# The last level of a block solve: GpSimd adds the unit matrix instead of 16 identity products on TensorE

## The chip, the cores and the metric

The kernel runs on one core of a Trainium2 chip. The metric is the device time of one launch in microseconds (us), lower is better. One core has TensorE (PE, with its weight loads shown as PEld), VectorE (DVE), ScalarE (ACT), GpSimd (POOL) and SyncE (SP), each with its own in-order queue of instructions, and they synchronise by semaphores.

## The reference

A two-layer decoder over 32 items (batch entries) of 128 tokens by 128 channels. Only one part touches the change: the second layer's linear attention with 16 heads of 64 channels. In it the recurrence over the 64 tokens of a chunk,

```
S = S * a_t[:, :, None]
kTS = einsum('bd,bde->be', k_t, S)
S = S + (b_t * k_t)[:, :, None] * (v_t - kTS)[:, None, :]
```

is not run token by token. The kernel solves the unit lower triangular system (I - N) W = V per head, with N strictly lower triangular of size 64, as a product of factors: W = (I + N^32) (I + N^16) ... (I + N) V. That is six levels, k = 0 to 5. Level k needs N^(2^k); step X{k} makes the next power by squaring and step W{k} multiplies W by (I + N^(2^k)).

## The kernel before, in words

The kernel has three blocks one after the other (first layer, a quantised feed-forward part that finds its scales, second layer). The third block, from about 1170 us to the end, holds the change. Two items are in flight, called lane 0 and lane 1, half a round apart; 16 rounds serve 32 items. Each lane has its own buffers, 4 PSUM banks and semaphores. Every engine's queue is written out in full by a fixed list of 0s and 1s (`CSLOTS`) that says which lane gives its next stage; no scheduler decides anything at run time. So an engine that waits in one lane's stage also holds up the other lane's stages behind it.

The 16 heads are handled as 8 pairs, and `tiles()` gives 16 products of 64x64 per step. An f32 product is two matrix instructions in the profile, each with its own weight load, so 16 products are rows with x32.

Where the change sits, in the order of TensorE's queue in lane 0: X4 (line 1203, last squaring), then for lane 1 the norm's product (L1010), W4 and KmT (L1217, L1221), for lane 1 one filler product (L353, `keep_warm`, products with no use that keep TensorE busy) and "conv" (L1109), then A (L1238), W5 (L1227 and L1229), then lane 1's "alpha" (L1115, L1117), which waits for DVE's L1512 ("c4m"). In lane 1 the order is X4, W4, KmT, lane 0's "fc" (L1306), A, lane 0's "pj" (L1312), W5, lane 0's "y" (L1100), fillers, and lane 0's last norm (L1007), which waits for DVE's L1600.

At levels 0 to 4 GpSimd forms I + N^(2^k) in SBUF (`with_identity`, L995, buffer `TI`) and TensorE multiplies once. At level 5 TensorE multiplies twice into one PSUM sum: N^32 times W (L1227) and the identity times W (L1229).

DVE's work in lane 1 that belongs to "conv" and "inner" is a convolution with 4 taps over three buffers: L1481 (`tensor_scalar`, SBUF to SBUF, two per-partition scalars, x3), L1507 ("zm", reads PSUM), L1483 (`scalar_tensor_tensor`, two SBUF tensors in, x6), then L1512. GpSimd's other instruction in this block is L458 ("Kbd", once per item).

Of the kernel before, what the change touches and what calls it, by code (L numbers as in the profile page):

```python
# [32 lines left out]
DK = 64  # L33
# [117 lines left out]
def decoder(nc, a):  # L151
    with ExitStack() as ctx:
# [12 lines left out]
        ident = sb("ident", [P, P])  # L165
# [70 lines left out]
        for s in range(LANES):  # L236
            n = Lane()
# [108 lines left out]
        mm = nc.tensor.matmul  # L346
# [122 lines left out]
        def sigmoid(act, ph, it, s, name, cols):  # L469
# [17 lines left out]
        LEVELS = 6  # L487
        y_pe, y_act, y_dve, y_pool = attention_steps("y")
# [12 lines left out]
             "Qd0", "Qd1", "Km0", "Kp0", "Km1", "Kp1", "t2", "cc", "dd", "Mm", "P0", "cV0", "cV1", *[f"X{k}" for k in range(LEVELS - 1)],  # L501
             "AT0", "AT1", "S", "ve", "f", "ON0", "ON1", "xs", "lng", "qmask", "yq", *y_dve, "ys", "lny", "fr2",
             *[f"ls{i}" for i in range(1, 6)], "lx", "lnf"],
            [*[f"TI{k}" for k in range(LEVELS - 1)], *y_pool])


        w_raw = lane[0].Kbd[:, 0:2 * FT, :]
# [87 lines left out]
        pe_did, act_did, dve_did, pool_did, loaded, stored = ph.pe, ph.act, ph.dve, ph.pool, ph.loaded, ph.stored  # L595
# [383 lines left out]
        def tiles():  # L979

            for j in range(NP // 2):
                for p in (j, j + NP // 2):
                    for lo, hi in halves:
                        other = (DK - lo, P + DK - hi) if p >= NP // 2 else (lo, hi)
                        yield p, slice(lo, hi), slice(*other)

        def groups():

            order = list(tiles())
            return [order[k:k + 4] for k in range(0, len(order), 4)]  # L990
# [30 lines left out]
        with nc.Block() as block:  # L1021
# [27 lines left out]
            @block.gpsimd  # L1049
            def _(pool):  # L1050
                def advance(s, it, stage):
                    n = lane[s]
                    if stage == "T0":
                        pool.wait_ge(pc.act[s], pc.AC.upto(it, "T0"))
                        with_identity(pool, it, s, 0)
                    for k in range(LEVELS - 2):
                        if stage == f"X{k}":
                            pool.wait_ge(pc.act[s], pc.AC.upto(it, f"X{k}"))
                            pool.wait_ge(pc.dve[s], pc.DV.upto(it, f"X{k}"))
                            if k > 0:  # L1060
                                pool.wait_ge(pc.pe[s], pc.PE.upto(it, f"W{k - 1}"))
                            with_identity(pool, it, s, k + 1)
                    if stage == "yKbd":
                        pool_attention(pool, pc, it, s, "y", pc.PE.upto(it, "O1"))
                in_rounds(pool, advance, CSLOTS["pool"])

            @block.tensor
            def _(pe):
                def advance(s, it, stage):
                    n, b = lane[s], lane[s].bank  # L1070
# [4 lines left out]
                    def dve_did(name):  # L1075
                        pe.wait_ge(pc.dve[s], pc.DV.upto(it, name))
# [14 lines left out]
                    if stage == "h":  # L1091
                        keep_warm(b[3], CWARM["h"])
                        pe.wait_ge(pc.loaded[s], 16 * C_LOADS * (it + 1))
                        for j in range(FT):
                            last = mm(b[3][:, j * P:(j + 1) * P], w1_q[:, j, :], n.xq[:, 0, :], start=True, stop=True)
                        last.then_inc(pf.pe[s], pf.PE.step(s, "h"))
                    if stage == "y":
                        pe.wait_ge(pf.dve[s], pf.DV.upto(it, "hq2"))
                        for j in range(FT):
                            last = mm(b[3][:, 0:P], w2_q[:, j, :], n.hq[:, j * P:(j + 1) * P], start=(j == 0), stop=(j == FT - 1))  # L1100
# [20 lines left out]
                    if stage == "F":  # L1121
                        keep_warm(b[0], CWARM["F"])
                        act_did("aE1")
                        for i in range(2):
                            act_did(f"aL{i}")
                            for p in range(4 * i, 4 * i + 4):
                                last = mm(pair_out(p, 2), n.B[:, p, :], since[:, :], start=True, stop=True)  # L1127
# [7 lines left out]
                    def held():  # L1135
                        pe.sem_inc(pe_passed, 1)

                    def solve_out(p, at, bank, col=0, width=DK):
                        first = (p % 4) * width + col
                        return n.psum[at, bank + p // 4, first:first + DK]  # L1140

                    if stage == "ssq":
# [3 lines left out]
                        for odd in range(2):  # L1146
                            for j in range(4):
                                p = 2 * j + odd
                                last = mm(b[0][QR * j:QR * (j + 1), 0:2 * P], hsel[:, p, :], squares[:, p, :, :], start=(odd == 0), stop=(odd == 1))
# [38 lines left out]
                    for k in range(LEVELS):  # L1188

                        PT, W = (n.PT0, n.PT1)[k % 2], n.W if k > 0 else n.cV[:, 0, :, :]  # L1190
                        if stage == f"X{k}":
                            if k == 0:
                                act_did("T0")
                            else:
                                act_did(f"X{k - 1}")
                                dve_did(f"X{k - 1}")
                            held()
                            for group in groups():
                                if k < LEVELS - 2:
                                    for p, src, dst in group:  # L1200
                                        mm(solve_out(p, dst, 2, 0, P), PT[src, p, 1, :], PT[src, p, 0, :], start=True, stop=True)  # L1201
                                for p, src, dst in group:
                                    last = mm(solve_out(p, dst, 2, DK, P), PT[src, p, 0, :], PT[src, p, 1, :], start=True, stop=True)  # L1203
                            last.then_inc(pc.pe[s], pc.PE.step(s, f"X{k}"))
                        if stage == f"W{k}":
                            if k == 0:
                                dve_did("cV1")
                            elif k < LEVELS - 1:
                                act_did(f"W{k - 1}")
                            else:  # L1210
                                act_did("KmT")
                                dve_did(f"X{k - 1}")
                            if k < LEVELS - 1:
                                pe.wait_ge(pc.pool[s], pc.PO.upto(it, f"TI{k}"))
                                held()
                                for p, src, dst in tiles():
                                    last = mm(solve_out(p, dst, 0), n.TI[src, k % 2, p, :], W[src, p, :], start=True, stop=True)  # L1217
                                last.then_inc(pc.pe[s], pc.PE.step(s, f"W{k}"))
                                if k == LEVELS - 2:
                                    for p, src, dst in tiles():  # L1220
                                        last = mm(solve_out(p, dst, 0, 4 * DK), n.Km[src, p, 0:DK], ident[src, src], start=True, stop=True)  # L1221
                                    last.then_inc(pc.pe[s], pc.PE.step(s, "KmT"))
                                continue
                            held()
                            for group in groups():
                                for p, src, dst in group:
                                    mm(solve_out(p, dst, 0), PT[src, p, 1, :], W[src, p, :], start=True, stop=False)  # L1227
                                for p, src, dst in group:
                                    last = mm(solve_out(p, dst, 0), ident[src, src], W[src, p, :], start=False, stop=True)  # L1229
                            last.then_inc(pc.pe[s], pc.PE.step(s, f"W{k}"))  # L1230
                    if stage == "A":
                        act_did(f"X{LEVELS - 2}")
                        dve_did(f"X{LEVELS - 2}")
# [481 lines left out]
```

## Time and profile before

| what | value |
|---|---|
| time of 3 runs | 2942.89 us median (2939.81 to 2944.56) |
| the profiled execution, its own time | 2953.11 us |
| its span in the trace | 2951.3 us |
| PE busy | 2614.6 us, 89% of the span (104.6 of 110.0 us from 2184 to 2294, a round of the third block) |
| DVE, ACT busy | 1669.5 us (57%), 1640.9 us (56%) |
| POOL busy | 305.0 us (10%), of it L995 202.7 us in 160 instructions |
| granted TensorE clock, mean | 0.98 |

Shares of busy time are means over stages; what ends a wait at one place is read from the rows. In such rows "idle before <- who" is the time the engine did nothing before the instruction and what released it; "issue" means that nothing in the profile held it, as when its next instructions had not arrived.

### The profile page before, as it was taken

How to read it: one execution, taken by the hardware profiler on the slowest of the kernel's cores; microseconds unless marked ns; L12 is line 12 of the kernel's file. 1: busy time of each engine (PE TensorE's matmuls, PEld its weight loads, DVE VectorE, ACT ScalarE, POOL GpSimd, SP SyncE). 2: the span in 40 equal slices, each digit the busy share in tenths (PEclk: the TensorE clock that was granted, in tenths of full speed). 3: DMA queues.
4: the chain of work that ended last, by engine and by line, in shares of the span. 5: the costliest groups of instructions: out<-in, count | busy, mean ns of one | idle time of the engine just before them, and what ended most of it. 6: DMA issues, size and time to landing. Idle time of an engine off the chain costs nothing.

```text
span 2951.3 us, 94478 instructions
## 1 busy us (share of the span) xinstructions
PE 2614.6 (89%) x41924; PEld 1885.5 (64%) x41928; DVE 1669.5 (57%) x3917; ACT 1640.9 (56%) x3841; POOL 305.0 (10%) x270
## 2 busy tenths in 40 slices
PE   3888888888888865999999999999999999998997
PEld 1665655566565543777776766777777777766775
DVE  3556656655665655456555465555556556555563
ACT  2655655655565532565565555555565565565563
POOL 0000000000000000111111111111111111111111
PEclk9999999999999986999999999999999999999999
DMA  3000000000000001000000000000000000000000
GB/s 98 6 8 6 6 9 7 6 6 8 6 6 9 6 22 29 6 6 8 7 6 8 7 6 8 7 6 8 7 5 8 7 6 8 7 5 8 7 6 4
DMA packets 50654, 29.21 MB, mean 10 GB/s; under 512 B 19792, under 2 KB 48528, under 8 KB 50256
## 3 DMA queue, kind: packets, MB, share of 16 engines
q1 hardware_dynamic: 50256, 23.25, 2.8%
q8 instruction: 330, 5.41, 0.8%
q14 instruction: 68, 0.56, 0.1%
HBM read 17.98 MB, written 5.24 MB: 8 GB/s over the span
## 4 chain that ended last, share of the span: by engine, by line
PE 47%; ACT 6%; DVE 5%; issue 2%; POOL 1%; DMA 0%; SPq 0%; POOLq 0%; DVEq 0%
PE bank L353 6%; PE bank L1087 4%; PE bank L1154 2%; PE bank L1117 2%; PE bank L1203 2%; PE bank L1284 2%; PE bank L1217 2%; PE bank L1127 2%; PE bank L1010 2%; PE bank L1201 2%; PE bank L388 2%; ACT zels L1335 1%; PE bank L1007 1%; PE bank L1252 1%; PE bank L371 1%
## 5 line engine op out<-in xcount | busy, mean ns | idle before, releaser
L353 PE MATMUL bank<-w_gate,ident 128*128 128x128 f32 (+3 forms) x1984 | 597.6, 389 | 0.6 <-issue 0.6
L353 PEld LDWEIGHTS bank<-w_gate,ident 128*128 128x128 f32 x1984 | 309.1, 192 | 76.0 <-issue 57.0
L458 POOL TENSOR_TENSOR Kbd<-kT,headmask 128x512 f32<-128x512 f32 x96 | 100.3, 1045 | 1919.8 <-DVE kT L436 1919.8
L441 DVE TENSOR_REDUCE m<-bank 128x4 f32<-128x512 f32 x384 | 262.1, 683 | 44.6 <-PE bank L378 24.1
L443 DVE TENSOR_TENSOR zels<-bank,m 128x512 f32<-128x512 f32 x384 | 265.6, 692 | 13.3
L419 ACT ACTIVATE zels<-zels 128x512 f32<-128x512 f32 x384 | 231.5, 627 | 69.8 <-DVE zels L443 66.7
L388 PE MATMUL bank<-ident,zels 128*128 128x128 f32 x1536 | 233.0, 282 | 40.3 <-ACT zels L419 38.7
L995 POOL TENSOR_TENSOR PT<-zels,unit 128x512 f32<-128x512 f32 x160 | 202.7, 1271 | 634.4 <-ACT zels L1335 513.6
L388 PEld LDWEIGHTS bank<-ident,zels 128*128 128x128 f32 x1536 | 173.8, 143 | 78.5 <-ACT zels L419 62.6
L422 ACT ACTIVATE PT<-bank 128x512 f32<-128x512 f32 x384 | 203.8, 592 | 16.2 <-PE bank L388 16.2
L1335 ACT ACTIVATE PT<-bank 128x512 f32<-128x512 f32 x256 | 148.7, 601 | 93.0 <-PE bank L1117 42.6
L1335 ACT ACTIVATE zels<-bank 128x512 f32<-128x512 f32 (+1 forms) x256 | 142.3, 572 | 95.8 <-PE bank L1186 58.8
L1335 ACT ACTIVATE W<-bank 128x512 f32<-128x512 f32 x192 | 114.5, 596 | 117.1 <-PE bank L1229 58.8
L465 ACT ACTIVATE rstd<-bank,eps 128x128 f32<-128x128 f32 x288 | 105.4, 366 | 129.0 <-PE bank L1010 89.3
L1563 DVE COPY zels<-bank 128x512 f32<-128x512 f32 (+1 forms) x160 | 101.4, 633 | 120.9 <-PE bank L1203 119.4
L1203 PE MATMUL bank<-zels 64*64 64x64 f32 x5120 | 153.9, 222 | 0.1
L1201 PE MATMUL bank<-zels 64*64 64x64 f32 x4096 | 135.4, 225 | 1.8 <-issue 1.0
L1203 PEld LDWEIGHTS bank<-zels 64*64 64x64 f32 x5120 | 131.4, 137 | 4.0
L371 PE MATMUL bank<-Kbd,qT 32*128 32x512 f32 x768 | 110.0, 641 | 18.3 <-POOL Kbd L458 18.3
L394 PE MATMUL bank<-PT,V 128*32 128x128 f32 x3072 | 115.5, 279 | 7.0 <-ACT PT L422 5.4
L1201 PEld LDWEIGHTS bank<-zels 64*64 64x64 f32 x4096 | 112.9, 137 | 12.7 <-issue 5.2
L1217 PE MATMUL bank<-W,PT 64*64 64x64 f32 x4096 | 91.1, 224 | 9.1 <-issue 8.1
(283 smaller groups left out, 5075.9 us busy)
## 6 DMA issues: line engine op xcount, KB each, us to landing
ctxT<-in_ctxT_dram SPq DMA_DIRECT2D x64, 48.0 KB, 1.7
x<-in_xT_dram SPq DMA_DIRECT2D x32, 64.0 KB
x_after_cross_attention<-x SPq DMA_DIRECT2D x32, 64.0 KB, 1.6
h<-x_after_cross_attention SPq DMA_DIRECT2D x8, 256.0 KB, 2.9
xin<-x_after_cross_attention SPq DMA_DIRECT2D x32, 64.0 KB, 1.8
out_dram<-xn SPq DMA_DIRECT2D x32, 64.0 KB, 1.6
input_integers<-xq SPq DMA_DIRECT2D x8, 128.0 KB, 2.0
xq<-input_integers SPq DMA_DIRECT2D x32, 32.0 KB, 1.8
```

The costliest lines, as they stand in the source:

```text
L353: mm(bank[:, 0:cols], ident[:, :], w_gate[:, :, :].rearrange("p a b -> p (a b)")[:, 0:cols], start=True, stop=True)
L371: last = mm(b[u][:, :], n.qT[rows, :], n.Kbd[rows, 0:HU, :], start=True, stop=not masked)
L388: last = xp(b[u][:, j * P:(j + 1) * P], n.zels[:, u, j * P:(j + 1) * P], ident[:, :])
L419: act.activation(n.zels[:, u, :], n.zels[:, u, :], ACT.Exp, scale=ATT_SCALE).then_inc(ph.act[s], ph.AC.step(s, f"{t}P{u}"))
L422: act.activation(n.PT[:, u, :], b[u][:, :], ACT.Copy).then_inc(ph.act[s], ph.AC.step(s, f"{t}PT{u}"))
L441: dve.tensor_reduce(top, scores, AX_X, ALU.max).then_inc(ph.dve[s], ph.DV.step(s, f"{t}max{u}"))
L443: dve.tensor_tensor(n.zels[:, u, :].rearrange("p (h k) -> p h k", h=HU), scores, top.unsqueeze(2).broadcast_to([P, HU, P]), ALU.subtract). ...
L995: pool.tensor_tensor(n.TI[:, k % 2, :, :], (n.PT0, n.PT1)[k % 2][:, :, 1, :], unit[:, :].unsqueeze(1).broadcast_to([P, NP, DK]), ALU.add)\
L1201: mm(solve_out(p, dst, 2, 0, P), PT[src, p, 1, :], PT[src, p, 0, :], start=True, stop=True)
L1203: last = mm(solve_out(p, dst, 2, DK, P), PT[src, p, 0, :], PT[src, p, 1, :], start=True, stop=True)
L1217: last = mm(solve_out(p, dst, 0), n.TI[src, k % 2, p, :], W[src, p, :], start=True, stop=True)
L1335: ins = act.activation(out, src, func, **how)
```

## The change

GpSimd forms I + N^32 as well: its X4 stage, empty before, now waits for X4's two halves (ACT and DVE) and for W3, and adds the unit matrix. TensorE's W5 waits for that sum and does 16 products; the 16 products with the identity, and the grouping by fours, are gone.

```diff
-            [*[f"TI{k}" for k in range(LEVELS - 1)], *y_pool])
+            [*[f"TI{k}" for k in range(LEVELS)], *y_pool])
...
-                    for k in range(LEVELS - 2):
+                    for k in range(LEVELS - 1):
                         if stage == f"X{k}":
                             pool.wait_ge(pc.act[s], pc.AC.upto(it, f"X{k}"))
                             pool.wait_ge(pc.dve[s], pc.DV.upto(it, f"X{k}"))
...
-                                dve_did(f"X{k - 1}")
-                            if k < LEVELS - 1:
...
+                            pe.wait_ge(pc.pool[s], pc.PO.upto(it, f"TI{k}"))
                             held()
-                            for group in groups():
-                                for p, src, dst in group:
-                                    mm(solve_out(p, dst, 0), PT[src, p, 1, :], W[src, p, :], start=True, stop=False)
-                                for p, src, dst in group:
-                                    last = mm(solve_out(p, dst, 0), ident[src, src], W[src, p, :], start=False, stop=True)
+                            for p, src, dst in tiles():
+                                last = mm(solve_out(p, dst, 0), n.TI[src, k % 2, p, :], W[src, p, :], start=True, stop=True)
                             last.then_inc(pc.pe[s], pc.PE.step(s, f"W{k}"))
```

On GpSimd, in the third block, two rounds of the loop (Kbd is L458 in either lane; PT_0 holds TI of lane 0):

```order
 L458 TENSOR_TENSOR Kbd_1<-kT_1,headmask 128x512
-L995 TENSOR_TENSOR PT_0<-zels_0,unit 128x512 x5
+L995 TENSOR_TENSOR PT_0<-zels_0,unit 128x512 x6
 L458 TENSOR_TENSOR Kbd_0<-kT_0,headmask 128x512
-L995 TENSOR_TENSOR PT_1<-zels_1,unit 128x512 x5
+L995 TENSOR_TENSOR PT_1<-zels_1,unit 128x512 x6
 L458 TENSOR_TENSOR Kbd_1<-kT_1,headmask 128x512
```

Each item has one more addition, last of its row of six, and nothing has changed places.

On TensorE, lane 0 from A to lane 1's alpha (L1238 is A, and L1228 the same line of the changed kernel; L1227 and L1229 are W5 before, L1215 is W5 now; bank1 belongs to lane 1):

```order
-L1238 MATMUL bank0<-Qd_0,Km_0 64x64 x32
-L1227 MATMUL bank0<-W_0,zels_0 64x64 x4
-L1229 MATMUL bank0<-W_0,ident 64x64 x4
-L1227 MATMUL bank0<-W_0,zels_0 64x64 x4
-L1229 MATMUL bank0<-W_0,ident 64x64 x4
-L1227 MATMUL bank0<-W_0,zels_0 64x64 x4
-L1229 MATMUL bank0<-W_0,ident 64x64 x4
-L1227 MATMUL bank0<-W_0,zels_0 64x64 x4
-L1229 MATMUL bank0<-W_0,ident 64x64 x4
+L1228 MATMUL bank0<-Qd_0,Km_0 64x64 x32
+L1215 MATMUL bank0<-W_0,PT_0 64x64 x16
 L1115 MATMUL bank1<-bias3,ones_bf 128x512 x2
```

The 32 products of W5 have become 16, in the same place between A and lane 1's alpha.

## Rows read from the trace of the kernel before

**Rows 1.** Chain of work that ended last, 1853 to 1870: start us, us, what

```profile
1854.07 0.86 DVE h L1481 x3
1856.88 0.21 DVE h L1512
1857.14 0.39 PE bank L1115 x2
```

**Rows 2.** Timeline around lane 0's W5: start us, us, engine, line, what, count, [idle before]

```profile
1852.98 0.69 PE L1217 MATMUL bank<-W,PT 64*64 64x64 f32 x32
1853.61 0.36 ACT L1335 ACTIVATE zels<-bank 128x256 f32<-128x256 f32 x1
1855.70 0.30 PE L1227 MATMUL bank<-W,zels 64*64 64x64 f32 x8
1856.52 0.30 PE L1229 MATMUL bank<-W,ident 64*64 64x64 f32 x8
1856.80 0.28 DVE L1512 TENSOR_TENSOR h<-zels 128x128 f32<-128x128 f32 x1
1857.14 0.39 PE L1115 MATMUL bank<-bias,ones_bf 32*128 32x512 bf16 x2 [0.33 <-DVE h L1512]
```

**Rows 3.** Timeline at an earlier level, lane 0: GpSimd behind ACT

```profile
1840.38 0.58 ACT L1335 ACTIVATE zels<-bank 128x512 f32<-128x512 f32 x1
1841.04 1.27 POOL L995 TENSOR_TENSOR PT<-zels,unit 128x512 f32<-128x512 f32 x1 [1.96 <-ACT zels L1335]
```

**Rows 4.** Timeline where L458 meets DVE, and line L1483 (ns min/median/max)

```profile
1924.62 1.65 DVE L1483 SCALAR_TENSOR_TENSOR h<-xpad,conv_w,h 128x128 f32<-128x128 f32 x3
1924.78 1.08 POOL L458 TENSOR_TENSOR Kbd<-kT,headmask 128x512 f32<-128x512 f32 x1 [24.84 <-DVE kT L436]
...
L1483 DVE SCALAR_TENSOR_TENSOR h<-xpad,conv_w,h x288: 337/346/1130, 1148.7 to 2856.7; 128x128 f32<-128x128 f32 x144
```

**Rows 5.** Groups by line: count | busy us, mean ns of one | idle before

```profile
L995 POOL TENSOR_TENSOR PT<-zels,unit 128x512 f32<-128x512 f32 x160 | 202.7, 1271 | 634.4 <-ACT zels L1335 513.6 <-DVE zels L1563 79.0 <-issue 41.8
L1481 DVE TENSOR_SCALAR h<-xpad,conv_w,conv_b 128x128 f32<-128x128 f32 x96 | 27.4, 342 | 0.6
L1520 DVE TENSOR_SCALAR PT<-PT 128x512 f32<-128x512 f32 x64 | 27.2, 425 | 16.1 <-ACT PT L1335 16.0
L816 DVE TENSOR_SCALAR zels<-bank 128x512 f32<-128x512 f32 x32 | 22.1, 692 | 29.7 <-PE bank L690 29.7
L796 DVE TENSOR_SCALAR h<-zels 128x128 f32<-128x128 f32 x32 | 7.3, 227 | 50.9 <-ACT zels L474 50.9
L910 DVE TENSOR_SCALAR h<-h,q_in 128x512 f32<-128x512 f32 x8 | 3.9, 486 | 6.5 <-DMA h<-x_after_cross_attention 6.3 <-DVE bias L906 0.2
```

**Rows 6.** Timeline around lane 1's W5

```profile
1904.81 0.69 DVE L1590 TENSOR_TENSOR h<-h 128x512 f32<-128x512 f32 x1 [1.67 <-ACT h L1335]
1909.03 0.29 DVE L1600 SCALAR_TENSOR_TENSOR x<-h,x 128x128 f32<-128x128 f32 x1
1909.38 0.49 PE L1007 MATMUL bank<-x,center 128*128 128x128 f32 x2
```

**Rows 7.** Timeline, the round after, where instructions came late

```profile
1897.58 0.80 PE L353 MATMUL bank<-w_gate,ident 128*128 128x384 f32 x2 [0.62 <-issue]
1963.39 0.86 DVE L1481 TENSOR_SCALAR h<-xpad,conv_w,conv_b 128x128 f32<-128x128 f32 x3
1967.16 0.33 PE L1229 MATMUL bank<-W,ident 64*64 64x64 f32 x3 [1.04 <-issue]
1967.42 0.39 PE L1115 MATMUL bank<-bias,ones_bf 32*128 32x512 bf16 x2
2074.72 0.35 DVE L1481 TENSOR_SCALAR h<-xpad,conv_w,conv_b 128x128 f32<-128x128 f32 x1
```

**Rows 8.** Waits of PE, 1185 to the end: us in total, times, longest

```profile
PE bank L1217 <- issue: 8.1, 4, 2.3
...
PE bank L1227 <- issue: 3.4, 4, 1.1
PE bank L1229 <- issue: 3.2, 5, 1.0
```

**Rows 9.** Stretches: length, PE, PEld, DVE, ACT, POOL busy, PEclk, DMA share, GB/s

```profile
1557.00:1560.40 3.40, 3.37 (x71) 2.53 (x69) 0.69 (x1) 1.06 (x3) 0.18 (x1) 0.51 0.02 5
...
1970.00:1973.40 3.40, 3.40 (x38) 2.10 (x37) 1.45 (x5) 2.83 (x6) 0.00 (x0) 0.50 0.00 0
```

More of the change, by code:

```diff
@@ L1211, in advance @@
                                 act_did("KmT")
-                                dve_did(f"X{k - 1}")
-                            if k < LEVELS - 1:
-                                pe.wait_ge(pc.pool[s], pc.PO.upto(it, f"TI{k}"))
-                                held()
-                                for p, src, dst in tiles():
[L1217 to L1224, printed above, removed]
-                            for group in groups():
-                                for p, src, dst in group:
-                                    mm(solve_out(p, dst, 0), PT[src, p, 1, :], W[src, p, :], start=True, stop=False)
-                                for p, src, dst in group:
-                                    last = mm(solve_out(p, dst, 0), ident[src, src], W[src, p, :], start=False, stop=True)
-                            last.then_inc(pc.pe[s], pc.PE.step(s, f"W{k}"))
+                            pe.wait_ge(pc.pool[s], pc.PO.upto(it, f"TI{k}"))
+                            held()
+                            for p, src, dst in tiles():
+                                last = mm(solve_out(p, dst, 0), n.TI[src, k % 2, p, :], W[src, p, :], start=True, stop=True)
+                            last.then_inc(pc.pe[s], pc.PE.step(s, f"W{k}"))
+                            if k == LEVELS - 2:
+                                for p, src, dst in tiles():
+                                    last = mm(solve_out(p, dst, 0, 4 * DK), n.Km[src, p, 0:DK], ident[src, src], start=True, stop=True)
+                                last.then_inc(pc.pe[s], pc.PE.step(s, "KmT"))
                     if stage == "A":
```

## The prediction

> **What bounds the kernel now.** I read the chain of work that ended last first. In lane 0's half of a round it does not run through W5: it leaves TensorE at lane 1's norm, goes through DVE's L1481 x3, L1507, L1483 x6 and L1512, and comes back to TensorE at L1115 [rows 1]. The reader should see that the three L1481, 0.86 us, are on it. Then I read the timeline: W5 runs on TensorE from 1855.70 to 1856.82, and TensorE then idles 0.33 us for L1512 before L1115 [rows 2]. The waits of PE show the second thing that matters: it is also held by "issue", instructions that come late, at L1227 and L1229 among others [rows 8], as at 1967.16 [rows 7]. So in some rounds L1512 releases L1115, in others TensorE's own stream does. I measured from the end of L1512 to the start of L1115 in the 16 rounds: 0.06 us where DVE sets it (1857.08 to 1857.14) up to 1.38 us, mean 0.66 us. 1966.40 to 1967.42, 1.02 us, is one of the late ones; its L1512 follows L1481 by the same 2.73 us as at 1854.07.
>
> **What is removed.** 16 products with the identity per item, 32 items. W5 now takes 1.12 us from its first to its last end (1855.70 to 1856.82); 16 products of W4 take 0.69 us [rows 2], and by starts the saving is 0.47 us. 32 x 0.47 = 15.0 us of TensorE work. How much of it reaches the end?
>
> Lane 1: behind W5 come y and fillers, then L1007 at 1909.38, released by DVE's L1600, which ends at 1909.32 [rows 6]. That DVE chain does not wait for W5. TensorE only gets there earlier and idles: worth 0.
>
> Lane 0: the gain shows only where L1115 is not set by L1512, at most 0.47 us a round. Summed over the 16 rounds it would be 5.7 us, if nothing else changed.
>
> **What is added.** One GpSimd addition per item, 1271 ns [rows 5], and W5's wait for it. It starts when X4's later half is copied. GpSimd starts 0.08 us behind ACT (1840.96 to 1841.04) [rows 3]. In lane 0 ACT's half ends at 1853.97, so the addition runs 1854.05 to 1855.32, and W5 (1855.70) doesn't wait for it: 0.3 us to spare, and behind that 0.33 us of idle and the 0.47 us saved. In lane 1 DVE is the later half, ending 1903.14 (1904.81 less the idle of 1.67) [rows 6]; W5 is 3.5 us later. The waiting cost of W5 is 0 in both lanes. Behind W5 on TensorE stands lane 1's alpha, and it would pay if this were wrong. On GpSimd only L458 stands behind, 20 us or more later.
>
> **What the addition meets.** This is the term that decides. In lane 0 the addition runs 1854.05 to 1855.32, and DVE's three L1481 start at 1854.07 [rows 2, 1]: with 0.08 us behind ACT (77 ns when read finely) GpSimd starts 13 ns before the first, and I find this same offset in all 16 rounds. The trace shows once a round what GpSimd can do to DVE: three L1483 take 1.65 us instead of 0.87 when L458 starts at 1924.78, between the first and the second; the second takes up to 1130 ns instead of 346 [rows 4]. It ends 0.15 us after L458 ends. The first, which started 0.16 us before L458, loses nothing. DVE instructions that read PSUM run at their usual time beside GpSimd.
>
> No row shows a `tensor_scalar` from SBUF in this place. The bounds: below, nothing; above, held as L1483 is, until the addition's end plus 0.15 us. Then L1481's first ends at 1855.32 + 0.15 = 1855.47 in place of 1854.41, a delay of 1.06 us. Which? A `tensor_scalar` of 512 columns takes 425 ns from SBUF and 692 ns from PSUM [rows 5], so from SBUF it moves two elements in the time of one, and takes as much out of SBUF per cycle as L1483 with its two tensors. That is the row nearest to it, and I take the upper bound. L1481 itself fits this: 227 ns for 128 columns, plus twice the 61 ns that one per-partition scalar costs (486 less 425), gives 349 for 342 measured [rows 5]. A single-speed run with one 60 ns charge fits as well, so it is not proven.
>
> The Trainium skill ("SBUF — State Buffer", Who interferes with whom) says that `tensor_scalar` from SBUF can enter a mode with both ports, that GpSimd shares the second pair, and that the one that issues second is fully blocked; by it the sum is that of the upper bound, and by a reading in which only two-tensor instructions contend it would be that of the lower. No run here shows the case of `tensor_scalar` yet.
>
> With the delay, L1512 is late by 1.06 us in every lane-0 half, since L1507 and L1483 follow L1481 without idle. L1115 then starts 0.06 us behind L1512 in all 16 rounds. Against now: 1.06 + 0.06 - 0.66 = 0.46, times 16 = **+7.3 us**. The 0.47 us that W5 saves is in there: it all turns into idle. The convolution's end holds lane 1's alpha, and all behind it in TensorE's queue moves.
>
> **What the idle does to the clock.** TensorE would then be idle from W5's end (1856.82 - 0.47 = 1856.35) to L1115 (1857.14 + 1.06 = 1858.20), 1.85 us in one piece. In the third block's rounds there are four waits as long, all at L1217 for "issue" (8.1 us in 4, 1.8 to 2.3 us each) [rows 8], and behind each of the four the granted clock is 0.5, 1.2 GHz, for 3.4 us (of the four, the one that ended at 1555.12 has its row) [rows 9]. Of the shorter idles, 0.35 to 1.4 us, one of about twenty was followed by the low clock: that of 1967.16, 1970.0 to 1973.4 [rows 7, 9]. Its price is read there: from L1481 to L1481 the round takes 111.33 us (1963.39 to 2074.72) against 109.32 for the round before (1854.07 to 1963.39) [rows 7]. Of the 2.01 us between them 0.96 is the later L1115 (4.03 against 3.07 us behind L1481), and the round before had 0.51 us of late instructions at 1897.58. That leaves 2.01 - 0.96 + 0.51 = 1.56 us for one low stretch. How many come? Rounds in which W5 or A also waits for late instructions have the idle in two pieces; I count 9 of those and 7 with one piece. I take most of the 7 and half of the 9, 10 in all, less the 1 there already: 9 x 1.56 = **+14 us**. Bounds: 0 to 15 such stretches, 0 to 23 us.
>
> **Late instructions.** A whole round has 4382 TensorE instructions in the trace, and 4254 after. The waits for "issue" come at multiples of 256 of them, where the stretch before is dense, so the places move. Putting the new multiples on the old waits gives 23 us over 16 rounds for 26 now, of which the part that counts outside A and W5 is 15 before and 16 after. I take 0, and +-5 us for the range.
>
> **The sum.** 7.3 + 14 + 0 = +21 us: 2953.1 becomes 2974 for a profiled execution. That execution is 10.2 us above the median of the runs (2942.9), and I move the sum there: **2964 us**.
>
> **The rivals.**
> 1. *Held, but the clock stays up* (fewer than 4 low stretches): +7 to +13, 2950 to 2956 us. For it: nineteen of twenty idles under 1.4 us did nothing. Against: 1.85 us is as long as those that did. Chance 0.15.
> 2. *Not held*, faster: L1481 runs beside GpSimd as DVE's PSUM readers do. The gain is what lane 0 keeps, 5.7 us of the 15.0, perhaps with the low stretch at 1970 gone: 2942.9 - 6 = 2937 us, with the moved waits 2932 to 2942. It decides at one point, whether `tensor_scalar` SBUF to SBUF is held. For it: the duration fits single speed too. Chance 0.2.
> 3. *W5 waits for GpSimd*: if the addition loses the race by those 13 ns and goes second, it ends up to 0.3 us later, about when W5 wants it; DVE's second L1481 is then held instead of the first, 0.2 us more. +10 on the forecast's side, 2955 to 2978. I count it with the forecast.
>
> **How the numbers follow.** Forecast (held, 4 to 15 low stretches) 0.65, 2952 to 2974 us. Range over all: 2937 to 2975. A change of less than 0.2% (5.9 us) cannot be told from none by this measurement, so "faster" is below 2937.0 and "slower" above 2948.8. Faster: half of rival 2, 0.10. Same: the other half and a little of rival 1, 0.13. Slower: 0.77.
>
> **What would show it.** L1481 in lane 0's half: the first near 1400 ns beside a L995, the other two at 342. L1512 to L1115 0.06 us everywhere. L1115's idle <- DVE L1512 about 16 times 1.8 us. PEclk of 0.5 behind it in more than half the rounds. L1007's idle in lane 1 up by 0.4 us with no gain. If L1481 keeps 342 ns the prediction is wrong at its root; if it is long and the clock stays at 1, by the second term alone.

## The result, and the profile after

The changed kernel takes 2975.48 us (median of 6 runs, 2963.00 to 2979.97) beside 2944.09 us for the kernel before (6 runs, 2939.81 to 2953.55). The ratio is **1.0098, 95% interval 1.0073 to 1.0123**: slower by 1%, 29 us by the ratio. The profiled execution took 2979.97 us with a span of 2978.2, 26.9 us more than the span before.

Head of the page of the changed kernel (busy us, share of the span, instructions; then the granted TensorE clock in tenths over 40 slices):

```profile
span 2978.2 us, 92498 instructions
PE 2630.1 (88%) x40904; PEld 1886.5 (63%) x40904; DVE 1684.5 (57%) x3917; ACT 1641.7 (55%) x3841; POOL 346.0 (12%) x302
PEclk9999999999999987999999999999999999999998
```

Fewer products on TensorE, and more time. The page hardly shows why: shares of busy time have stayed, and of the clock's slices in the third block only the last has changed, from 9 to 8. The lines do. The groups that answer to [rows 5], columns as there; L1471 is the L1481 of before:

```profile
L995 POOL TENSOR_TENSOR PT<-zels,unit 128x512 f32<-128x512 f32 x192 | 243.6, 1272 | 698.2 <-ACT zels L1325 535.3 <-DVE zels L1553 121.1 <-issue 41.8
L1471 DVE TENSOR_SCALAR h<-xpad,conv_w,conv_b 128x128 f32<-128x128 f32 x96 | 43.3, 505 | 0.6
```

GpSimd has 32 more additions of the old length. The 96 L1471 went from 27.4 to 43.3 us, which a mean of 505 ns hides: it is 16 instructions at about 1345 ns and 80 near the old length (332 to 346 ns). The timeline of lane 0's half in one round, GpSimd's row first, then DVE and TensorE (start us, us, [idle before]); it answers to [rows 2] and [rows 1]:

```profile
1523.12 1.28 POOL L995 TENSOR_TENSOR PT<-zels,unit 128x512 f32<-128x512 f32 x1 [1.18 <-ACT zels L1325]
...
1523.13 1.35 DVE L1471 TENSOR_SCALAR h<-xpad,conv_w,conv_b 128x128 f32<-128x128 f32 x1
...
1524.76 0.65 PE L1215 MATMUL bank<-W,PT 64*64 64x64 f32 x32
1527.20 0.39 PE L1115 MATMUL bank<-bias,ones_bf 32*128 32x512 bf16 x2 [1.80 <-DVE h L1502]
```

L995 starts 0.01 us before the first L1471, which then lasts until 1524.48, 0.08 us after L995's end. Read finely, this is so in all 16 rounds: L995 first by 9 to 13 ns, the first L1471 1336 to 1349 ns long. The first and the last pieces of the chain there:

```profile
1523.13 1.86 DVE h L1471 x3
...
1526.95 0.21 DVE h L1502
1527.16 0.05 issue
1527.20 0.39 PE bank L1115 x2
```

L1471 x3 is 1.86 us where it was 0.86 [rows 1]. W5 ends at 1525.41 (1524.76 + 0.65), 1.80 us before L1115 can start: what W5 saves is part of that idle. The waits of PE, third block, with what answers to [rows 8] (us in total, times, longest):

```profile
PE bank L1115 <- DVE h L1502: 17.4, 16, 1.8
...
PE bank L1215 <- issue: 7.4, 7, 1.9
...
PE bank L1228 <- issue: 4.3, 4, 1.3
PE bank L1219 <- issue: 3.0, 3, 1.4
```

L1115 now waits for DVE in all 16 rounds. What stands behind that wait is the larger loss. The stretches behind L1115 in two rounds (length, busy us of PE, PEld, DVE, ACT, POOL, then the granted clock), as [rows 9]:

```profile
1519.00:1527.70 8.70, 6.80 (x239) 5.52 (x240) 6.43 (x18) 5.40 (x14) 2.54 (x2) 1.00 0.04 11
1527.70:1534.50 6.80, 6.80 (x42) 3.40 (x43) 3.45 (x11) 3.67 (x7) 0.00 (x0) 0.50 0.01 2
1534.50:1541.30 6.80, 6.62 (x131) 5.86 (x130) 0.96 (x2) 4.57 (x9) 0.00 (x0) 1.00 0.01 2
...
1415.10:1421.90 6.80, 6.80 (x43) 3.40 (x42) 3.83 (x11) 3.67 (x7) 0.00 (x0) 0.50 0.00 1
```

The clock is at 1.2 GHz (0.50) for 6.8 us from 0.5 us after L1115's start. Such a stretch follows L1115 in 9 of the 16 rounds, 8 of them 6.8 us long and one 3.4. Before, it did in two: the 3.4 us at 1970 of [rows 9], and one of 6.8 us in the first round of the block, 1.8 us behind the start of L1115 at 1189.93:

```profile
1191.70:1198.50 6.80, 6.80 (x49) 4.58 (x48) 2.62 (x6) 3.38 (x7) 0.00 (x0) 0.50 0.01 2
```

The price of a stretch in the changed kernel is read from the starts of L1471:

```profile
1410.12 1.34 DVE L1471 TENSOR_SCALAR h<-xpad,conv_w,conv_b 128x128 f32<-128x128 f32 x1
...
1523.13 1.35 DVE L1471 TENSOR_SCALAR h<-xpad,conv_w,conv_b 128x128 f32<-128x128 f32 x1
...
2537.19 1.34 DVE L1471 TENSOR_SCALAR h<-xpad,conv_w,conv_b 128x128 f32<-128x128 f32 x1
...
2647.01 1.34 DVE L1471 TENSOR_SCALAR h<-xpad,conv_w,conv_b 128x128 f32<-128x128 f32 x1
```

The first pair is a round with the stretch at 1415.10: 113.01 us. The second has none: 109.82 us. Both have about 1 us of late instructions, so I put the difference, 3.2 us, down to one low-clock stretch.

### The profile page after: what moved, and what is told of

Read it like the earlier page. It is cut to its first block, busy times and chain, and to the rows that moved or that the text cites. A ratio compares the mean times of both kernels' runs of the same rounds, so it can differ in the third digit from the quotient of the medians.

```text
span 2978.2 us, 92498 instructions
## 1 busy us (share of the span) xinstructions
PE 2630.1 (88%) x40904; PEld 1886.5 (63%) x40904; DVE 1684.5 (57%) x3917; ACT 1641.7 (55%) x3841; POOL 346.0 (12%) x302
## 4 chain that ended last, share of the span: by engine, by line
PE 45%; DVE 7%; ACT 7%; issue 2%; POOL 1%; DMA 0%; SPq 0%; POOLq 0%; DVEq 0%
PE bank L353 5%; PE bank L1087 4%; PE bank L1117 2%; PE bank L1154 2%; PE bank L1203 2%; PE bank L1127 2%; PE bank L1274 2%; PE bank L1010 2%; PE bank L1201 2%; PE bank L388 2%; PE bank L1215 2%; ACT zels L1325 1%; PE bank L1007 1%; PE bank L1242 1%; PE bank L371 1%
## 5 line engine op out<-in xcount | busy, mean ns | idle before, releaser
L353 PE MATMUL bank<-w_gate,ident 128*128 128x128 f32 (+3 forms) x1984 | 606.7, 394 | 0.0
L995 POOL TENSOR_TENSOR PT<-zels,unit 128x512 f32<-128x512 f32 x192 | 243.6, 1272 | 698.2 <-ACT zels L1325 535.3
L458 POOL TENSOR_TENSOR Kbd<-kT,headmask 128x512 f32<-128x512 f32 x96 | 100.5, 1047 | 1839.0 <-DVE kT L436 1839.0
L1215 PE MATMUL bank<-W,PT 64*64 64x64 f32 x5120 | 113.9, 224 | 8.4 <-issue 7.4
```

The source lines that it names most:

```text
L353: mm(bank[:, 0:cols], ident[:, :], w_gate[:, :, :].rearrange("p a b -> p (a b)")[:, 0:cols], start=True, stop=True)
L995: pool.tensor_tensor(n.TI[:, k % 2, :, :], (n.PT0, n.PT1)[k % 2][:, :, 1, :], unit[:, :].unsqueeze(1).broadcast_to([P, NP, DK]), ALU.add)\
```

## The experiments

To compare the traces I took three quantities from each, in the third block between the first and the last round's L1481 (15 rounds): how far L1115 starts behind L1481 (mean of 16), the time at the low clock, and the sum of TensorE's waits for late instructions ("issue", waits over 0.15 us, as the rows of waits count them; the expectations on record, counted a little more widely, have 24.5 us for before and 14.3 for x1). The runs:

| kernel | ratio to before | 95% interval | L1115 behind L1481, us | low clock, us | late instructions, us | first to last L1481, us |
|---|---|---|---|---|---|---|
| before | 1 | | 3.72 | 23.9 | 23.9 | 1666.1 |
| changed | 1.0098 | 1.0073 to 1.0123 | 4.07 | 64.9 | 16.4 | 1688.0 |
| x1, products removed, nothing added | 0.9956 | 0.9940 to 0.9971 | 3.25 | 6.8 | 13.4 | 1648.3 |
| x2, addition added, nothing removed | 1.0036 | 1.0022 to 1.0049 | 4.15 | 54.6 | 23.6 | 1687.0 |
| x3, changed, fillers in the idle | 1.0018 | 1.0008 to 1.0028 | 4.59 | 6.8 | 15.2 | 1665.6 |
| x4, DVE adds the unit matrix | 0.9966 | 0.9954 to 0.9978 | 3.30 | 17.1 | 11.9 | 1648.5 |
| x5, half the addition | 1.0003 | 0.9990 to 1.0015 | 3.60 | 17.1 | 14.7 | 1658.4 |
| x6, the change in lane 1 alone | 1.0001 | 0.9990 to 1.0011 | 3.80 | 0 | 22.4 | 1656.2 |
| x7, before, instructions shifted | 0.9983 | 0.9971 to 0.9994 | 3.62 | 6.8 | 17.1 | 1654.2 |
| x8, changed, shifted | 1.0092 | 1.0067 to 1.0117 | 4.07 | 64.9 | 15.6 | 1687.1 |
| x9, x1 shifted | 0.9964 | 0.9950 to 0.9978 | 3.28 | 10.2 | 21.2 | 1653.4 |
| x10, x4 shifted | 0.9962 | 0.9950 to 0.9975 | 3.35 | 13.7 | 22.5 | 1655.6 |
| x11, addition in two pieces | 1.0063 | 1.0047 to 1.0079 | 3.96 | 34.1 | 14.3 | 1670.4 |

The last four columns are of one profiled execution each, and executions of a kernel differ (x2's was the longest of its eight, 2975.45 us with a median of 2960.16, and x11's the shortest of its four, 2960.35 with 2969.10), so ratios are compared with ratios and traces with traces.

**x1: the products removed, and nothing else.** W5 leaves out the identity products; no sixth addition takes their place, so the unit part of the last level is missing.

```diff
                                 for p, src, dst in group:
-                                    mm(solve_out(p, dst, 0), PT[src, p, 1, :], W[src, p, :], start=True, stop=False)
-                                for p, src, dst in group:
-                                    last = mm(solve_out(p, dst, 0), ident[src, src], W[src, p, :], start=False, stop=True)
+                                    last = mm(solve_out(p, dst, 0), PT[src, p, 1, :], W[src, p, :], start=True, stop=True)
```

> The kernel before with W5's 16 identity products left out and no addition on GpSimd, so W5 multiplies by N^32 alone (the last factor's unit part is missing). My theory (the removed products are worth little because lane 1 waits for DVE and lane 0 gives back at most 0.47 us a round): 2 to 8 us below before, ratio 0.997 to 0.999, L1481 at 342 ns. Rival theory (the removed products are worth their 15 us of TensorE work and the loss lies elsewhere): ratio near 0.995.

Measured: 0.9956 (0.9940 to 0.9971), 13 us faster. That is the rival's 0.995 and not the theory's 0.997 to 0.999. L1115 moved forward by 0.47 us on the mean (3.72 to 3.25), which over 16 rounds is 7.5 us, near the 5.7 of the prediction's working. The rest of the gain goes with less low clock and fewer late instructions in the same stretch. x9 and x7 ask whether that was luck.

**x2: the addition and its wait, with all 32 products of W5 kept.** The sum is formed and waited for, but not read.

```diff
...
-                    for k in range(LEVELS - 2):
+                    for k in range(LEVELS - 1):
...
+                            pe.wait_ge(pc.pool[s], pc.PO.upto(it, f"TI{k}"))
                             held()
```

> The kernel before with GpSimd's sixth addition and W5's wait for it, but W5 still does all 32 products and does not read the sum. My theory (the addition holds DVE's first L1481 for 1 us and that sets L1115): L1481 1345 ns once a round, L1115 4.07 us behind L1481 as in the changed kernel, TensorE's idle before it 0.47 us shorter, so fewer stretches of low clock: ratio 1.003 to 1.009. Rival theory (the loss comes from W5 with half the products and its moved instructions, not from the addition): ratio 1.000 with L1115 where it was.

Measured: 1.0036. The first L1481 (L1482 in this kernel) is 1339 to 1355 ns long in all 16 rounds, so the addition does this alone. Beside x1 this is the most telling pair: taking the products away from the kernel before gives 0.44%, and taking them away from x2 gives the changed kernel, whose ratio to before (taken in another comparison) is 0.6% above x2's. I read this as the products covering part of TensorE's idle time: the waits before L1115 are up to 1.32 us here and up to 1.80 us without them. How much of the 0.6% is the clock can't be told from x2's one trace, which is that of its slowest execution.

**x3: the changed kernel with six filler units ahead of lane 1's alpha**, where TensorE idles.

```diff
-                        keep_warm(b[1], CWARM["alpha"])
+                        keep_warm(b[1], 6 if s == 1 else 0)
```

> The changed kernel with 6 units of filler products (about 1.3 us) on TensorE ahead of lane 1's alpha, in the place where it idles for DVE's held convolution. My theory (two terms: the hold of 0.35 us a round net, and the low clock that the idle brings): the fillers leave L1115 at 4.07 us behind L1481, the stretches of half clock behind it go from 9 to 0 or 1, and the time falls by 20 to 27 us, to 1.001 to 1.004 of before. Rival theory (the low clock costs nothing of its own, and DVE's delay is the whole loss): the time stays at 1.01 of before.

Measured: 1.0018. The hold is untouched, and TensorE still can't begin L1115 before DVE's L1502. A round of x3:

```profile
1519.63 1.27 POOL L995 TENSOR_TENSOR PT<-zels,unit 128x512 f32<-128x512 f32 x1 [1.17 <-ACT zels L1325]
1519.64 1.85 DVE L1471 TENSOR_SCALAR h<-xpad,conv_w,conv_b 128x128 f32<-128x128 f32 x3
...
1523.70 0.39 PE L1115 MATMUL bank<-bias,ones_bf 32*128 32x512 bf16 x2 [0.30 <-DVE h L1502]
```

The idle of 1.80 us is 0.30 us, L1115 starts at the same distance of 4.06 us from L1471 there, and no low clock follows. In other rounds, where instructions came late, the fillers stand in the way and push L1115 to 5 us and more (mean 4.59, not the 4.07 I had expected). Even so, 58 us of low clock are gone and with them four fifths of the loss: from 1.0098 to 1.0018. Work with no use was added, L1115 came later, and the kernel was faster: this shows the clock's share.

**x4: DVE adds the unit matrix while it copies X4 out of PSUM**, both halves; ACT's copy of X4 and GpSimd's sixth addition are gone, and W5 does 16 products.

```diff
...
-                        then(dve.tensor_copy(new, out), stage)
+                        if k == LEVELS - 2:
...
+                            then(dve.tensor_tensor(new, out, unit[:, :].unsqueeze(1).unsqueeze(1).broadcast_to([P, 2, 4, DK]), ALU.add), stage)
+                        else:
+                            then(dve.tensor_copy(new, out), stage)
```

> The identity products gone as in the changed kernel, but no GpSimd addition: DVE copies both halves of X4 out of PSUM with the unit matrix added (one tensor_tensor of 512 columns, PSUM and one SBUF input), and ACT's half of that copy is gone. My theory: DVE has room there in both lanes (0.3 us and 1.3 us idle behind it), L1481 stays at 342 ns, and the time is that of x1_removed_only within 3 us, 0.996 to 0.999 of before. Rival theory (the longer copy on DVE delays A and L1481): 1.000 to 1.003.

Measured: 0.9966 (0.9954 to 0.9978). This version beats both kernels. The addition costs what a plain copy of the same size costs; columns as in [rows 5], that copy in the changed kernel behind it:

```profile
L1555 DVE TENSOR_TENSOR zels<-bank,unit 128x512 f32<-128x512 f32 x32 | 22.0, 686 | 19.9 <-PE bank L1203 19.9
```
```profile
L1553 DVE COPY zels<-bank 128x512 f32<-128x512 f32 x128 | 87.9, 686 | 98.1 <-PE bank L1203 96.4
```

686 ns each. L1481 (L1473 here) is back at 335 to 348 ns. DVE copies both halves in one such instruction; before, it copied one half in 420 ns and ACT the other. So DVE gives 0.27 us more an item, and x4 still comes within 0.1% of x1.

**x5: the addition over half the tiles.** W5 reads the other half as an earlier level left it.

```diff
-            pool.tensor_tensor(n.TI[:, k % 2, :, :], (n.PT0, n.PT1)[k % 2][:, :, 1, :], unit[:, :].unsqueeze(1).broadcast_to([P, NP, DK]), ALU.add)\
+            tl = NP // 2 if k == LEVELS - 1 else NP
+            pool.tensor_tensor(n.TI[:, k % 2, 0:tl, :], (n.PT0, n.PT1)[k % 2][:, 0:tl, 1, :], unit[:, :].unsqueeze(1).broadcast_to([P, tl, DK]), ALU.add)\
```

> The changed kernel, but GpSimd's last addition covers only 4 of the 8 tiles (256 of 512 columns); W5 reads the other 4 as an earlier level left them. Theory (the first L1481 is held until the addition ends, plus 0.08 us, and the low clock comes only behind the long idles): the addition takes about 0.65 us, the first L1481 about 0.73 us instead of 1.345, L1502 ends about 3.40 us behind it instead of 4.01. The longest idle before L1115 falls from 1.80 to about 1.2 us, and the low stretches behind L1115 go almost all. From the kernel with the products removed alone (0.9956): +0.15 to 0.3 us of offset x 16 = 2 to 5 us, and one or two stretches at 1.6 to 3.2 us each: 0.996 to 1.000. Rival A (any idle of about 1 us brings the low clock): most of the stretches stay, 1.004 to 1.007. Rival B (the hold is a fixed price of a meeting, not the rest of the addition): L1481 stays at 1.3 us and the ratio at 1.0098.

Measured: 1.0003, at the upper end of the theory's 0.996 to 1.000, far from both rivals. The timeline:

```profile
1520.61 0.73 POOL L996 TENSOR_TENSOR PT<-zels,unit 128x256 f32<-128x256 f32 x1 [1.17 <-ACT zels L1326]
1520.62 1.31 DVE L1472 TENSOR_SCALAR h<-xpad,conv_w,conv_b 128x128 f32<-128x128 f32 x3
...
1524.14 0.39 PE L1116 MATMUL bank<-bias,ones_bf 32*128 32x512 bf16 x2 [1.17 <-DVE h L1503]
```

The half takes 0.73 us (I had expected 0.65), the first L1472 0.80 us (0.73 expected), and again it ends 0.08 us behind GpSimd's end. The hold is the rest of the addition and not a fixed price. The idle before L1116 is 1.17 us here, and low-clock stretches follow it in 4 rounds of 16 in place of 9 (the first included).

**x6: the change in lane 1 alone.** Lane 0 keeps its 16 identity products and has five additions, the fifth of which counts for two in the semaphore.

```diff
...
-                    for k in range(LEVELS - 2):
+                    for k in range(LEVELS - 1 if s == 1 else LEVELS - 2):
...
-                            if k < LEVELS - 1:
+                            if k < LEVELS - 1 or s == 1:
```

> The kernel before, with the change made in lane 1 alone: there GpSimd adds the unit matrix for the last level and W5 does 16 products; lane 0 keeps its 16 identity products and has no sixth addition. Theory: the addition of lane 1 meets no L1481 of either lane (L1481 stays at 346 ns throughout), and the 0.47 us that W5 saves there ends as idle before L1007, so the ratio is 1.000, give or take 0.002 for late instructions that come at other places. Rival (the removed products of lane 1 are worth their time): -0.3 to -0.47 us x 16 = -5 to -7.5 us, 0.9975 to 0.998. Rival 2 (some of the loss is in lane 1, through GpSimd beside other DVE work): 1.002 or more.

Measured: 1.0001. L1481, min/median/max in ns:

```profile
L1481 DVE TENSOR_SCALAR h<-xpad,conv_w,conv_b x96: 335/341/347, 1147.5 to 2843.3; 128x128 f32<-128x128 f32 x96
```

Nothing is held, and no gain shows (the interval is 0.9990 to 1.0011, 3 us either way): the removed products of lane 1 are worth about 0, as the prediction's working had it from L1007 [rows 6], and the loss is lane 0's.

**x7 and x8: before and changed, with 128 TensorE instructions put in once** ahead of the third block's first product, where TensorE idles 11.7 us.

```diff
                         keep_warm(b[3], CWARM["h"])
+                        for _ in range(32 if s == 0 and it == 0 else 0):
+                            mm(b[3][0:DK, 0:DK], ident[0:DK, 0:DK], ident[0:DK, 0:DK], start=True, stop=True)
```

> The kernel before, with 32 products of 64x64 (128 TensorE instructions) put in once, ahead of the third block's first product, where TensorE idles 11.7 us for a DMA. They cost nothing there; they move every later TensorE instruction by half of 256. Theory (TensorE's waits for late instructions come at multiples of 256 instructions, and count where the stretch before is dense): the waits of the third block move to other places, their sum may go from 24.5 us to anything between 14 and 28 us and with it some low-clock stretches; the time changes by up to 10 us either way (0.9965 to 1.0035). Rival (the waits belong to places in the program, not to the count): the same waits at the same lines, ratio 1.000 within 0.001.

Measured: 0.9983. The waits for late instructions have moved: before, the largest was L1217 with 8.1 us in 4 waits, up to 2.3 us [rows 8]; in x7 the two largest entries, and L1217's own, are these (L1229 and L1240 are the L1227 and L1238 of before, and L1219 its L1217):

```profile
PE bank L1229 <- issue: 4.0, 5, 1.1
PE bank L1240 <- issue: 3.1, 5, 1.0
...
PE bank L1219 <- issue: 0.6, 1, 0.6
```

So the waits move with the count of instructions and don't belong to places in the program, and the kernel takes 5 us less when they fall elsewhere (2 to 9 by the interval), although the 128 instructions are not free where they stand. I had taken them for hidden in the idle; but TensorE begins them only at 1136.36, and they take 7.06 us, so 11.71 us of idle became 7.49 + 7.06 us, 2.8 us more. The same place before, then in x7:

```profile
1139.84 0.61 PE L1095 MATMUL bank<-xq,w_q 128*128 128x128 bf16 x4 [11.71 <-DMA mask_u<-in_query_mask_dram]
```
```profile
1136.36 7.06 PE L1094 MATMUL bank<-ident 64*64 64x64 f32 x64 [7.49 <-PEq L926]
1143.35 0.61 PE L1097 MATMUL bank<-xq,w_q 128*128 128x128 bf16 x4
```

The four shifted kernels all carry this, so each is best compared with x7. Any comparison of kernels that differ in instructions carries the places of the late instructions as an unknown.

> The changed kernel with the same 32 products put in once ahead of the third block. Theory: L1481's hold stays (first 1345 ns, L1115 4.07 us behind it), the late instructions come in other rounds, so another selection of rounds has the idle before L1115 in one long piece; the number of low-clock stretches behind L1115 stays between 7 and 12 and the ratio to the kernel before between 1.006 and 1.012. Rival (the loss was luck of the places): below 1.004.

Measured: 1.0092, as for the changed kernel, and 1.0109 times x7. Its loss is no luck of the places: 64.9 us of low clock, with 9 stretches behind L1115 again, and L1115 at 4.07 us in all rounds.

**x9 and x10: x1 and x4 with the same 128 instructions.**

> The kernel with the 32 identity products of a round left out and no sixth addition (the unit part of the last level is missing, as in x1), with 128 TensorE instructions put in once ahead of the third block. It tells how much of x1's 0.9956 was the removed work and how much the places of the late instructions. Theory (the removed products are worth 5 to 8 us, and the rest of x1's 13 us came from late instructions and low-clock stretches that happened to be few, 14.3 us and 6.8 us against 24.5 and 23.9 before): the ratio stays below 1 but moves towards 0.998, 0.996 to 0.999. Rival (the removed products are worth 13 us whatever the places): 0.9956 within 0.001.

> The kernel in which DVE adds the unit matrix while it copies X4 out of PSUM (x4), with the same 128 instructions put in once. If x4's gain holds at other places of the late instructions, the ratio lies between 0.995 and 0.999; if it was luck of the places, at 1.000 or above.

Measured: 0.9964 and 0.9962. Against the kernel before both gains hold, and x9 lies where theory and rival overlap. The kernel that differs from x9 by the removed products alone is x7, though: 0.9964 / 0.9983 = 0.9981, 5.6 us. Both ratios have their noise and come from different comparisons (together about 0.0018, so 0 to 11 us). That is the 5.7 us of the prediction's working, where x1 gave 13 us (9 to 18). So the worth of the removed products depends on where the late instructions fall, or the two are noise about some 9 us; these runs can't tell. x10 beside x7 is 0.9979, 6 us faster.

**x11: the sixth addition in two pieces**, 64 and 448 columns.

```diff
+            f = 1 if k == LEVELS - 1 else 0
+            if f:
+                pool.tensor_tensor(n.TI[:, k % 2, 0:f, :], (n.PT0, n.PT1)[k % 2][:, 0:f, 1, :], unit[:, :].unsqueeze(1).broadcast_to([P, f, DK]), ALU.add)
+            pool.tensor_tensor(n.TI[:, k % 2, f:, :], (n.PT0, n.PT1)[k % 2][:, f:, 1, :], unit[:, :].unsqueeze(1).broadcast_to([P, NP - f, DK]), ALU.add)\
```

> The changed kernel, with GpSimd's sixth addition in two pieces, the first of 64 columns, the second of the other 448, so that in lane 0 GpSimd is between two instructions when DVE has begun its three L1481. Theory (GpSimd holds a DVE instruction until its own ends, and one that DVE has begun first runs through): the first L1481 is held for the small piece alone, about 0.35 to 0.5 us, the second until the large piece ends, plus 0.08 us, so the three end at about the same place as in the changed kernel or up to 0.3 us later (2.0 to 2.3 us behind the start of the first against 1.86), L1115 stands 4.1 to 4.4 us behind L1481 and the ratio is 1.008 to 1.014. Rival (whoever comes first keeps the port for its whole group: DVE's three run through once the small piece has ended, and GpSimd waits): the three end by 1.2 us, the large piece is long (1.9 us or more), W5 waits for it, and the ratio is below 1.006.

Measured: 1.0063.

```profile
1523.93 0.32 POOL L997 TENSOR_TENSOR PT<-zels,unit 128x64 f32<-128x64 f32 x1 [1.18 <-ACT zels L1328]
1523.94 1.75 DVE L1474 TENSOR_SCALAR h<-xpad,conv_w,conv_b 128x128 f32<-128x128 f32 x3
1524.21 1.14 POOL L998 TENSOR_TENSOR PT<-zels,unit 128x448 f32<-128x448 f32 x1
```

Read finely, the first L1474 takes 0.39 us and ends 0.08 us after the small piece; it then runs through although the large piece has begun. The second takes 1.18 us and ends 0.08 us after the large piece; the third is at 0.33. DVE's three end at 1.75 us and not at 1.86, earlier than both theory (2.0 to 2.3) and the changed kernel. The mechanism came out as the theory said and not as the rival did (the large piece is not delayed, and W5 doesn't wait for it), its sizes did not: DVE uses the gap between two GpSimd instructions, and the ratio (1.0047 to 1.0079) is below the range expected. L1118 stands at 3.96 us, and the low clock in this trace is 34.1 us in place of 64.9, but the trace is that of the fastest of four executions.

## Why the prediction was right, and where it was off

**What held.** The direction, and each link of the mechanism. L1481's first instruction is held by GpSimd's addition (forecast near 1400 ns, measured 1345), always, as GpSimd wins by 9 to 13 ns; the others keep their length. L1115 starts 0.06 us behind L1512 in all 16 rounds. W5 does not wait for GpSimd. Lane 1 gives nothing (x6), and L1007's idle there has grown from 0.9 us in 1 wait to 8.6 us in 15. Low clock behind the new idle is the larger part (x3). The size came out at the edge: the median, 2975.48 us, is above the 2952 to 2974 of the forecast and half a us above the upper end of the whole range, 2975; the ratio on the 2942.9 of the prediction gives 2971.7. And L1115's idle is 17.4 us in 16 waits, 1.1 us on the mean and not 1.8, because in 8 rounds W5 or A had waited for late instructions before it. The rule of the Trainium skill ("SBUF — State Buffer", Who interferes with whom), that the `tensor_scalar` from SBUF shares a port pair with GpSimd and that the second to issue is blocked, agrees with the trace: 1345 ns in place of 346, and 344 to 348 in x1, where no addition runs.

**The hold.** Forecast +7.3 us. Measured: it ends 0.08 us after the addition and not 0.15, so the delay is 1.00 us and not 1.06; L1115 goes from 3.72 to 4.07 us behind L1481, 0.35 x 16 = 5.6 us.

**The clock: the term that was mis-sized.** It stood as "10 in all, less the 1 there already: 9 x 1.56 = +14 us". The count was nearly right: 9 rounds of 16, less 2 that were there already. The price was not. I read it from the 3.4 us at 1970 [rows 9], and 8 of the 9 stretches are 6.8 us long, at 3.2 us each. The trace of before had shown one such, at 1191.70, behind an idle of 1.09 us, and I had missed it, so "one of about twenty" should have been two. Its round took 112.91 us against 109.00 for the next, of which 0.74 us is the later L1115: 3.2 us, the price that was then paid. (The 0.51 us taken off for the wait at 1897.58 is 0.62 in its row [rows 7]; with it the 1.56 is 1.67.) Between the first and the last round's L1481 the low clock went from 23.9 to 64.9 us, and one stretch more lies behind the last. At 1.56 us for 3.4 us, or 3.2 us for 6.8 us, 0.46 to 0.47 us is lost for each us at the low clock: 41.0 x 0.47 = 19 us, and 3.2 us for the last round's, 22 us in all. The count rested on a guess, "most of the 7" rounds with the idle in one piece "and half of the 9" with two. It came to 5 of 8 and 4 of 8, near in number, but no rule that names the rounds: the 9 have idles before L1115 of 0.46, 0.66, 0.84, 1.01, 1.51, 1.61, 1.79, 1.80 and 1.80 us, and one of 1.79 us in one piece has none behind it:

```profile
2651.09 0.39 PE L1115 MATMUL bank<-bias,ones_bf 32*128 32x512 bf16 x2 [1.79 <-DVE h L1502]
```
```profile
2651.00:2657.80 6.80, 6.71 (x84) 4.46 (x88) 4.81 (x13) 4.83 (x10) 0.00 (x0) 1.00 0.01 2
```

**Late instructions.** Forecast 0 (+-5). The sum went from 23.9 to 16.4 us. By the fit below that gave back about 4 us, inside its bounds.

**Do the three terms carry it?** A fit of the 13 traces in the table gives the time from first to last L1481 as 1591.2 + 13.9 x (L1115 behind L1481) + 0.48 x (low clock) + 0.53 x (late instructions). x4 is off by 3.0 us, every other trace by 1.6 or less. The 0.48 is near the 0.46 that [rows 7] gave, and the 13.9 near the 15 rounds. From before to changed it gives 0.35 x 13.9 = 4.9, 41.0 x 0.48 = 19.7 and -7.5 x 0.53 = -4.0 us, together 20.6 of the 21.9 measured. From the changed kernel to x3 it gives 0.52 x 13.9 = 7.2, -58.1 x 0.48 = -27.9 and -1.2 x 0.53 = -0.6, together -21.3 for -22.4 measured. The fit is tested on the traces that it is made from, so it shows that the three terms suffice, not that no other would do. The remaining 5 us of the span are nearly all behind the last round's L1471 (103.8 us for 99.3), where the ninth low stretch lies; the kernel's last 13.5 us are at the low clock too, where before it was the last 1.7.

**The median.** The sum for a profiled execution was 2974, and it took 2980. I then took off 10.2 us, by which the profiled execution of before lay above its median; for the changed kernel that distance was 4.5 us. Of the 11.5 us between forecast and median, 5.8 are the sum and 5.7 this step. The clock's share differs from one execution to the next (2963.00 to 2979.97 us at mean clocks of 0.979 to 0.972), so such a distance isn't a constant to carry over.

**The rivals.** "Held, but the clock stays up" is x3 in effect, with 1.0018. "Not held" fell with L1481's 1345 ns. "W5 waits for GpSimd" never came up.

**Open.** What the removal alone is worth: 13 us in x1, 5.6 us from x7 to x9, where the working had 5.7. The traces of x1 and x9 show less low clock than before, 6.8 and 10.2 us for 23.9, but x7 has 6.8 us and x6 none with all or half of the products there; single profiled executions can't settle it. What decides, among rounds with the same idle, which one the low clock follows is open too.

## What to carry to other kernels

Before moving work to an idle engine, lay its instruction over the other engines' timeline: here GpSimd's 1.27 us cost DVE 1.00 us, since it began 0.01 us before an SBUF-to-SBUF `tensor_scalar` on the path. An addition that rides on DVE's copy out of PSUM added nothing to it here (686 ns with and without), and that was the better place for it. And price an idle of TensorE by what the clock does behind it, with the longest stretch it may bring: with the hold there, taking out 0.47 us of products in front of the wait made the kernel slower (1.0036 to 1.0098), and fillers in that place won back four fifths of the loss. Without the hold the same removal made it faster (x1).

## What was not expected of the hardware

- A held DVE instruction ends 0.08 us behind the GpSimd instruction, whatever the length of either wait: 0.39, 0.80, 1.18 and 1.35 us. L1483 in [rows 4] had shown 0.15.
- Between two GpSimd instructions in a row one DVE instruction gets through (x11).
- The low clock came in stretches of 3.4 and of 6.8 us behind idles of like length (1.61 us before the one of 3.4, 1.51 to 1.80 before four of 6.8), and the cost goes by the stretch's length, 0.46 to 0.48 us for each us.
- 128 instructions put in once, which themselves lengthened the way into the block by 2.8 us, made the same kernel 0.17% faster (0.9983, 0.9971 to 0.9994).
